# GpSimd's gathers in a factorization-machine kernel: the first layer's products in two halves with four gathers between, in place of eight gathers in a row

## The chip, the cores and the metric

One core of one Trainium2 chip runs the kernel. The metric is the device time of one execution in microseconds (us), lower is better. The kernel before took 1251.6 us, the median of 3 runs (1250.91 to 1251.73).

## The reference

A recommendation tower: 32 embedding lookups per sample, three layers of a compressed interaction network (each multiplies every field of the input with every row of the layer before, and contracts with weights), and a three-layer MLP on the sums.

```python
e = stack([tbl_f[ids[:, f]] for f in range(32)], axis=1)     # 2048 x 32 x 16
x0 = xk = e
for W in (W0, W1, W2):                                       # 32x32x64, 32x64x64, 32x64x64
    xk = relu(einsum('bmd,bhd,mhk->bkd', x0, xk, W))
    outs.append(sum(xk, axis=2))
h = concatenate([concatenate(outs, axis=1), dense_ctx], axis=1)   # 2048 x 208
h = maximum(h @ W_top1 + b_top1, 0)                          # 512
h = maximum(h @ W_top2 + b_top2, 0)                          # 256
y = h @ W_top3
```

All of it is in float32.

## The kernel before, in words

The batch of 2048 is cut into 32 steps of 64 samples. A step's embeddings are a matrix of 32 fields by 1024 columns (64 samples x 16 dimensions). Each engine has a program of its own, written out by hand, and the engines meet at semaphores alone; nothing reorders them.

**How a step's input comes in.** GpSimd (POOL) issues 16 indirect DMAs per step (`gather`, L248), each of which fetches 128 rows of the embedding table into `x_rows`, which is double-buffered. SyncE (SP) waits until all 16 have landed and stores them to a scratch in HBM (`store_x`, L183), twice. When the store has landed (L198) it loads the step back in three groups: `load_a` (L191: four DMAs of 512 KB, chunks 0 to 3 of `spread`), `load_q` (L214: four of 128 KB, the 32 fields four times over in `q_tile`, single-buffered) and `load_b` (L191: four of 512 KB, chunks 4 to 7 of `spread`). `spread` has three buffers. SP's loop is: the B of step s+1, then the store, A and q of step s+2.

**What is computed.** Layer 0 of a step multiplies chunks 0 to 3 of `spread` by `q_tile` into `p_l0` (`first_layer_products`, L260, two GpSimd instructions of two chunks each; ScalarE adds a fifth chunk, the squares, L327). TensorE contracts the five chunks (`layer0`), waiting for `l0_made` chunk by chunk. ScalarE copies the result through a ReLU into `xa` (L300) and `xb` (L309), two arrangements in PSUM, and into `x_s` (L318). VectorE multiplies `spread` with `xa` and `xb` in groups of one to three chunks (`products`, L497): 15 chunks for layer 1, then 15 for layer 2, with the sums over the 16 dimensions (L524) between. The 16th chunk of each of those layers is GpSimd's (`product`, L271). TensorE contracts them (L570).

**The order.** In round s of the loops, VectorE does layer 1 of step s, then layer 2 of step s-1. TensorE does the same, and puts layer 0 of step s+1 after the fourth chunk of layer 2 of step s-1. In every second round the MLP of an earlier pair of steps is put between TensorE's chunks (L632, L634, L644, L652), and ScalarE evicts it (`h`, L414 and L424; `y_row`, L433); its order in the round is `xb` of step s, the third layer's output, `h` of the MLP, `xa` of layer 1 of step s-1, squares, and so on.

**GpSimd's order** is what the change touches. Before the loop it gathers 44 times (`GATHERED_BEFORE`). Then, in round s, it does both instructions of the first layer's products of step s+1, four gathers (`THEN`), the layer-2 product of step s-1, four gathers, the layer-1 product of step s+1, and eight gathers. With 44 + 16 s gathered at the start of the round, the first four gathers of the round complete the rows of step s+2.

Of the kernel before, what the change touches and what calls it, by code (L numbers as in the profile page):

```python
# [6 lines left out]
ALU = mybir.AluOpType  # L7
# [10 lines left out]
Q = P // FIELDS  # L18
SB = 64
STEPS = BATCH // SB  # L20
COLS = SB * DIM
BLK = COLS // 2
XI = COLS // Q // DIM
TILES = BATCH // P
C0 = 5
# [21 lines left out]
L0_AFTER = 3  # L47


GATHERED_BEFORE, THEN = 44, 4  # L50

MLP_AFTER = 5, 10, 13
MLP_AFTER_LAST = 3, 9, 13
# [2 lines left out]
def gathers_before(s):  # L56

    return min(GATHERED_BEFORE + XI * s, XI * STEPS)
# [15 lines left out]
def pool_from(s, layer):  # L74


    if layer == 1:
        return max(0, 2 * s - 1)
    return min(2 * s + 2, 2 * STEPS - 1)


def build_kernel(nc, ids, table, first_row, dense_t, w0_mh, w0_hm, w1, w2, w_top1, b_top1, w_top2,
                 b_top2, w_top3, scratch, y):
    with ExitStack() as ctx:
        def sb(name, shape, dt=F32):
            return ctx.enter_context(nc.sbuf_tensor(name, shape, dt))
# [4 lines left out]
        def sem(name):  # L91
            return ctx.enter_context(nc.semaphore(name))
# [4 lines left out]
        spread = sb("spread", [P, 3, NT, COLS])  # L97
# [4 lines left out]
        p_l0 = sb("p_l0", [P, C0, COLS])  # L102
# [29 lines left out]
        q_loaded = sem("q_loaded")  # L132
        a_loaded = [sem(f"a_loaded{u}") for u in range(3)]
        b_loaded = [sem(f"b_loaded{u}") for u in range(3)]
        l0_made = sem("l0_made")
        squares_made = sem("squares_made")
        l0_used = sem("l0_used")
# [99 lines left out]
        @block.gpsimd  # L237
        def _(pool):
            def gather(n):

                s, i = divmod(n, XI)
                if n == 0:
                    pool.wait_ge(ids_ready, 1)
                if n == FIRST_IDS:
                    pool.wait_ge(ids_ready, 2)
                if i == 0 and s >= 2:
                    pool.wait_ge(x_stored, 32 * (s - 1))
                nc.gpsimd.indirect_dma_start(  # L248
                    out=x_rows[:, s % 2, i * DIM:(i + 1) * DIM], out_offset=None, in_=table,
                    in_offset=bass.IndirectOffsetOnAxis(ap=ids_s[:, n:n + 1], axis=0),  # L250
                ).then_inc(gathered[s % 2], 16)

            def first_layer_products(s):

                pool.wait_ge(q_loaded, 16 * Q * (s + 1))
                pool.wait_ge(a_loaded[s % 3], 16 * Q * (s // 3 + 1))
                pool.wait_ge(l0_used, C0 * s)
                q = q_tile[:].rearrange("p (o n) -> p o n", o=1).broadcast_to([P, 2, COLS])
                for c in 0, 2:
                    nc.gpsimd.tensor_tensor(p_l0[:, c:c + 2, :], spread[:, s % 3, c:c + 2, :],  # L260
                                            q, ALU.mult).then_inc(l0_made, 2)

            def product(s, layer):

                n = pool_from(s, layer)
                pool.wait_ge(x1s_ready if layer == 1 else x2s_ready, s + 1)
                if layer == 1:
                    pool.wait_ge(b_loaded[s % 3], 16 * Q * (s // 3 + 1))
                if n > 0:
                    pool.wait_ge(pool_used, n)  # L270
                nc.gpsimd.tensor_tensor(p_pool[:], spread[:, s % 3, POOL_CHUNK, :], x_s[:, layer - 1, :],  # L271
                                        ALU.mult).then_inc(pool_made, 1)

            def gathers(first, end):

                for n in range(min(first, XI * STEPS), min(end, XI * STEPS)):
                    gather(n)

            gathers(0, gathers_before(0))
            product(0, 1)  # L280
            for s in range(STEPS):
                n = gathers_before(s)
                if s + 1 < STEPS:
                    first_layer_products(s + 1)
                gathers(n, n + THEN)
                if s > 0:
                    product(s - 1, 2)
                gathers(n + THEN, n + 2 * THEN)
                if s + 1 < STEPS:
                    product(s + 1, 1)  # L290
                gathers(n + 2 * THEN, n + XI)
            product(STEPS - 1, 2)

        @block.scalar
# [433 lines left out]
```

## Time and profile before

| | |
|---|---|
| median of 3 runs | 1251.6 us |
| the profiled execution's own time | 1251.98 us |
| its span, first to last instruction | 1250.2 us |
| mean granted TensorE clock | 0.982 of 2.4 GHz |
| busy: TensorE / VectorE / ScalarE / GpSimd | 1127.5 / 1116.6 / 731.7 / 922.8 us |
| gathers (L248) | 512, 955 ns each |
| first layer's products (L260) | 62, 4564 ns each |
| GpSimd's product of layers 1 and 2 (L271) | 64, 2378 ns each |

The span leaves out 1.78 us of the execution's own time (1251.98 - 1250.2). Busy times are of instructions alone; an engine that waits for a semaphore is idle. GpSimd's gathers are the time in which it writes their descriptors; the transfers land later, without an engine's time.

### The profile page before, as it was taken

To read this page: it belongs to the slowest core of one execution; us is meant where nothing else is said; L and a number is where in the kernel's file an instruction comes from. 1 tells how busy PE (TensorE), PEld (TensorE's weight loads), DVE (VectorE), ACT (ScalarE), POOL (GpSimd) and SP (SyncE) were. 2 spreads that over 40 slices of the span, in tenths; PEclk is the share of its full clock that TensorE was granted. 3 is DMA by queue.
4 is the path that set the end of the run, shared out by engine and by line. 5 is a ranking of instruction groups with operands and counts; after the bars stand their busy time and mean duration, and the time that the engine had idled before them with its cause. 6 is when DMAs were issued, how large, how long until landed. Compare 5 with 4: busy or idle time off the path is not lost.

```text
span 1250.2 us, 14620 instructions
## 1 busy us (share of the span) xinstructions
PE 1127.5 (90%) x5312; PEld 395.0 (32%) x5312; DVE 1116.6 (89%) x519; ACT 731.7 (59%) x1361; POOL 922.8 (74%) x642
## 2 busy tenths in 40 slices
PE   0167999999999999999999999999999999999977
PEld 0012323323232333323233332323333332323324
DVE  0159999999999999999999999999999999999992
ACT  0036665766657566765656586565657666565661
POOL 6767888787878878788887878788787878785110
PEclk9888999999999999999999999999999999999988
DMA  5967887657677876666788665667866666777000
GB/s 119 187 132 140 164 164 156 136 117 149 126 148 155 165 145 124 140 126 139 150 164 162 125 145 120 141 133 162 164 142 139 124 142 124 154 163 160 2 1 1
DMA packets 76088, 167.25 MB, mean 134 GB/s; under 512 B 21648, under 2 KB 38944, under 8 KB 76016
## 3 DMA queue, kind: packets, MB, share of 16 engines
q1 hardware_dynamic: 59088, 161.95, 62.0%
q0 software_dynamic: 16384, 4.23, 3.4%
q8 instruction: 42, 0.69, 0.3%
q10 hardware_dynamic: 544, 0.14, 0.1%
q14 instruction: 30, 0.25, 0.1%
HBM read 157.86 MB, written 8.40 MB: 133 GB/s over the span
## 4 chain that ended last, share of the span: by engine, by line
PE 34%; issue 22%; DVE 18%; ACT 14%; another core or an unknown queue 12%; ACTq 0%; DVEq 0%
PE acc L570 30%; DVE p_dve L497 17%; ACT xb L309 10%; PE acc L644 3%; DVE z L524 1%; ACT h L414 1%; PE acc L652 1%; ACT out_l L393 1%; ACT x_s L318 1%; ACT xa L300 0%; PE acc L632 0%; PE acc L634 0%; ACT y_row L433 0%; ACTq L435 0%
## 5 line engine op out<-in xcount | busy, mean ns | idle before, releaser
L570 PE MATMUL acc<-p_dve,w_s 128*64 128x512 f32 x3840 | 868.6, 598 | 65.5 <-DVE p_dve L497 59.5
L248 POOL DMA_INDIRECT x_rows<-in_table,ids_s x512 | 489.2, 955 | 145.9 <-issue 132.9
L497 DVE TENSOR_TENSOR p_dve<-spread,xb 128x3072 f32<-128x3072 f32 (+2 forms) x224 | 565.8, 2583 | 9.8 <-issue 6.7
L497 DVE TENSOR_TENSOR p_dve<-spread,xa 128x2048 f32<-128x2048 f32 (+1 forms) x192 | 495.4, 2634 | 59.6 <-issue 59.6
L570 PEld LDWEIGHTS acc<-p_dve,w_s 128*64 128x64 f32 x3840 | 266.7, 137 | 621.7 <-issue 493.1
L309 ACT ACTIVATE xb<-acc 32x512 f32<-32x512 f32 x512 | 288.8, 564 | 109.4 <-DVE p_dve L497 98.5
L260 POOL TENSOR_TENSOR p_l<-spread,q_tile 128x2048 f32<-128x2048 f32 x62 | 281.3, 4564 | 9.4 <-DMA q_tile<-x_of_steps 8.0
L271 POOL TENSOR_TENSOR p_pool<-spread,x_s 128x1024 f32<-128x1024 f32 x64 | 152.2, 2378 | 137.7 <-ACT x_s L318 84.2
L300 ACT ACTIVATE xa<-acc 64x512 f32<-64x512 f32 x256 | 145.9, 570 | 147.2 <-PE acc L570 109.2
L570 PE MATMUL acc<-p_l,w_s 128*64 128x512 f32 (+1 forms) x640 | 148.9, 601 | 44.6 <-DVE p_l L543 44.6
L318 ACT ACTIVATE x_s<-acc 64x512 f32<-64x512 f32 x256 | 151.3, 591 | 3.8
L414 ACT ACTIVATE h<-acc,bt 128x128 f32<-128x128 f32 x64 | 18.2, 368 | 148.8 <-remote 132.4
L570 PEld LDWEIGHTS acc<-p_l,w_s 128*64 128x64 f32 (+1 forms) x640 | 43.4, 137 | 143.9 <-issue 143.9
L524 DVE TENSOR_REDUCE z<-out_l 128x32 f32<-128x512 f32 x96 | 62.3, 675 | 9.9 <-ACT out_l L393 9.9
L570 PE MATMUL acc<-p_pool,w_s 128*64 128x512 f32 x256 | 65.8, 592 | 0.0
L327 ACT ACTIVATE p_l<-q_tile 32x1024 f32<-32x1024 f32 x32 | 33.6, 1049 | 17.8 <-DMA q_tile<-x_of_steps 16.3
L644 PE MATMUL acc<-h,wt 128*128 128x128 f32 x256 | 34.6, 291 | 7.0 <-ACT h L414 7.0
L644 PEld LDWEIGHTS acc<-h,wt 128*128 128x128 f32 x256 | 31.4, 200 | 20.4 <-ACT h L414 18.8
L570 PEld LDWEIGHTS acc<-p_pool,w_s 128*64 128x64 f32 x256 | 18.4, 137 | 36.5 <-issue 36.5
L632 PE MATMUL acc<-z_all,wt 128*128 128x128 f32 x128 | 27.1, 294 | 3.1 <-ACT z_all L402 3.1
L393 ACT ACTIVATE out_l<-acc 128x512 f32<-128x512 f32 x32 | 19.1, 597 | 15.8 <-PE acc L570 15.3
L543 DVE TENSOR_TENSOR p_l<-spread,q_tile 128x2048 f32<-128x2048 f32 x2 | 4.5, 2288 | 26.6 <-DMA spread<-x_of_steps 26.6
(18 smaller groups left out, 159.8 us busy)
## 6 DMA issues: line engine op xcount, KB each, us to landing
spread<-x_of_steps SPq DMA_DIRECT2D x256, 512.0 KB
q_tile<-x_of_steps SPq DMA_DIRECT2D x128, 128.0 KB
x_rows<-in_table,ids_s POOLq DMA_INDIRECT x512
x_of_steps<-x_rows SPq DMA_DIRECT2D x64, 128.0 KB
w_s<-in_w SPq DMA_DIRECT2D x2, 512.0 KB
wt<-in_w_top SPq DMA_DIRECT2D x1, 512.0 KB
z_all<-in_dense_t ACTq DMA_DIRECT2D x16, 8.0 KB
wt<-in_w_top SPq DMA_DIRECT2D x1, 256.0 KB
```

The source lines that it names most:

```text
L248: nc.gpsimd.indirect_dma_start(out=x_rows[:, s % 2, i * DIM:(i + 1) * DIM], out_offset=None, in_=table, in_offset=bass.IndirectOffsetOnAxi ...
L260: nc.gpsimd.tensor_tensor(p_l0[:, c:c + 2, :], spread[:, s % 3, c:c + 2, :], q, ALU.mult).then_inc(l0_made, 2)
L271: nc.gpsimd.tensor_tensor(p_pool[:], spread[:, s % 3, POOL_CHUNK, :], x_s[:, layer - 1, :], ALU.mult).then_inc(pool_made, 1)
L300: last = nc.scalar.activation(xa[to:to + K, b * BLK:(b + 1) * BLK], acc[b * K:(b + 1) * K, :], ACT.Relu)
L309: last = nc.scalar.activation(xb[q * FIELDS:(q + 1) * FIELDS, b * BLK:(b + 1) * BLK], hi if q % 2 == 0 else lo, ACT.Relu)
L318: last = nc.scalar.activation(x_s[to:to + K, layer - 1, b * BLK:(b + 1) * BLK], acc[b * K:(b + 1) * K, :], ACT.Relu)
L327: nc.scalar.activation(p_l0[0:FIELDS, CP, :], q_tile[0:FIELDS, :], ACT.Square).then_inc(squares_made, 1)
L393: nc.scalar.activation(out_l[:, 2, :], acc2[:], ACT.Relu).then_inc(out_ready[2], 1)
L497: nc.vector.tensor_tensor(p_dve[:, to:to + n, :], spread[:, s % 3, tile:tile + n, :], over(x[:], n), ALU.mult).then_inc(dve_made, n)
L524: nc.vector.reduce_sum(z[:, s // 2 % 2, n, s % 2, :], out_l[:, n, :].rearrange("p (i d) -> p i d", d=DIM), AX_X).then_inc(z_made[n], 1)
L570: last = nc.tensor.matmul(acc[b * K:(b + 1) * K, :], w, prod[:, b * BLK:(b + 1) * BLK], start=start, stop=stop)
L644: last = nc.tensor.matmul(mlp_bank(t)[:, cols], wt2[:, k, cols], h1[:, k, :], start=(k == 0), stop=(k == H1 // P - 1))
```

## The change

The gathers ahead of the loop go from 44 to 40. In a round, the two instructions of the first layer's products stand apart, with four gathers between them, and the row of eight at the round's end becomes a row of four. The first half keeps the three waits; the second has none.

```diff
-GATHERED_BEFORE, THEN = 44, 4
+GATHERED_BEFORE, THEN = 40, 4
...
-            def first_layer_products(s):
-
-                pool.wait_ge(q_loaded, 16 * Q * (s + 1))
-                pool.wait_ge(a_loaded[s % 3], 16 * Q * (s // 3 + 1))
-                pool.wait_ge(l0_used, C0 * s)
+            def first_layer_products(s, c):
+
+                if c == 0:
+                    pool.wait_ge(q_loaded, 16 * Q * (s + 1))
+                    pool.wait_ge(a_loaded[s % 3], 16 * Q * (s // 3 + 1))
+                    pool.wait_ge(l0_used, C0 * s)
                 q = q_tile[:].rearrange("p (o n) -> p o n", o=1).broadcast_to([P, 2, COLS])
-                for c in 0, 2:
-                    nc.gpsimd.tensor_tensor(p_l0[:, c:c + 2, :], spread[:, s % 3, c:c + 2, :],
-                                            q, ALU.mult).then_inc(l0_made, 2)
+                nc.gpsimd.tensor_tensor(p_l0[:, c:c + 2, :], spread[:, s % 3, c:c + 2, :],
+                                        q, ALU.mult).then_inc(l0_made, 2)
...
                 if s + 1 < STEPS:
-                    first_layer_products(s + 1)
+                    first_layer_products(s + 1, 0)
                 gathers(n, n + THEN)
+                if s + 1 < STEPS:
+                    first_layer_products(s + 1, 2)
+                gathers(n + THEN, n + 2 * THEN)
                 if s > 0:
                     product(s - 1, 2)
-                gathers(n + THEN, n + 2 * THEN)
+                gathers(n + 2 * THEN, n + 3 * THEN)
                 if s + 1 < STEPS:
                     product(s + 1, 1)
-                gathers(n + 2 * THEN, n + XI)
+                gathers(n + 3 * THEN, n + XI)
```

GpSimd's program before, one round in the middle of the loop, from one first-layer product to the next (`p_l` is `p_l0`; waits in brackets are the semaphores that the instruction waits for):

```order
L260 TENSOR_TENSOR p_l<-spread,q_tile 128x2048 [waits a_loaded0,l0_used,q_loaded]
L260 TENSOR_TENSOR p_l<-spread,q_tile 128x2048
L248 DMA x_rows<-in_table,ids_s 128x16 x4
L271 TENSOR_TENSOR p_pool<-spread,x_s 128x1024 [waits pool_used,x2s_ready]
L248 DMA x_rows<-in_table,ids_s 128x16 [waits x_stored]
L248 DMA x_rows<-in_table,ids_s 128x16 x3
L271 TENSOR_TENSOR p_pool<-spread,x_s 128x1024 [waits pool_used,b_loaded0,x1s_ready]
L248 DMA x_rows<-in_table,ids_s 128x16 x8
L260 TENSOR_TENSOR p_l<-spread,q_tile 128x2048 [waits a_loaded1,l0_used,q_loaded]
```

The same round in the changed kernel:

```order
L260 TENSOR_TENSOR p_l<-spread,q_tile 128x2048 [waits a_loaded0,l0_used,q_loaded]
L248 DMA x_rows<-in_table,ids_s 128x16 x4
L260 TENSOR_TENSOR p_l<-spread,q_tile 128x2048
L248 DMA x_rows<-in_table,ids_s 128x16 x4
L271 TENSOR_TENSOR p_pool<-spread,x_s 128x1024 [waits pool_used,x2s_ready]
L248 DMA x_rows<-in_table,ids_s 128x16 [waits x_stored]
L248 DMA x_rows<-in_table,ids_s 128x16 x3
L271 TENSOR_TENSOR p_pool<-spread,x_s 128x1024 [waits pool_used,b_loaded0,x1s_ready]
L248 DMA x_rows<-in_table,ids_s 128x16 x4
L260 TENSOR_TENSOR p_l<-spread,q_tile 128x2048 [waits a_loaded1,l0_used,q_loaded]
```

Four of the eight gathers at the round's end now stand between the two halves of the product. The four that complete a step's rows still stand right ahead of the layer-2 product (the gather after that product, which waits for `x_stored`, is the first of the next step).

The end of GpSimd's program ahead of the loop and the first round, before:

```order
L248 DMA x_rows<-in_table,ids_s 128x16 [waits x_stored,ids_ready]
L248 DMA x_rows<-in_table,ids_s 128x16 x11
L271 ISA
L271 TENSOR_TENSOR p_pool<-spread,x_s 128x1024 [waits b_loaded0,x1s_ready]
L260 TENSOR_TENSOR p_l<-spread,q_tile 128x2048 [waits a_loaded1,l0_used,q_loaded]
L260 TENSOR_TENSOR p_l<-spread,q_tile 128x2048
L248 DMA x_rows<-in_table,ids_s 128x16 x4
```

And in the changed kernel:

```order
L248 DMA x_rows<-in_table,ids_s 128x16 [waits x_stored,ids_ready]
L248 DMA x_rows<-in_table,ids_s 128x16 x7
L271 ISA
L271 TENSOR_TENSOR p_pool<-spread,x_s 128x1024 [waits b_loaded0,x1s_ready]
L260 TENSOR_TENSOR p_l<-spread,q_tile 128x2048 [waits a_loaded1,l0_used,q_loaded]
L248 DMA x_rows<-in_table,ids_s 128x16 x4
L260 TENSOR_TENSOR p_l<-spread,q_tile 128x2048
L248 DMA x_rows<-in_table,ids_s 128x16 x4
```

Step 2's rows (the 48th gather) are complete after eight gathers of the first round instead of four. The programs of the other engines are the same in both kernels.

## Rows read from the trace of the kernel before

**Rows 1.** The page: busy time, share of the span, instructions.
```profile
PE 1127.5 (90%) x5312; PEld 395.0 (32%) x5312; DVE 1116.6 (89%) x519; ACT 731.7 (59%) x1361; POOL 922.8 (74%) x642
```
**Rows 2.** Waits of VectorE from 200 to 1100 us: total, times, longest.
```profile
DVE p_dve L497 <- issue: 34.2, 26, 2.3
```
**Rows 3.** Timeline of GpSimd, one round: start, duration, instruction [idle before <-releaser].
```profile
644.78 0.94 POOL L248 DMA_INDIRECT x_rows<-in_table,ids_s  x1 [0.31 <-issue]
645.74 9.06 POOL L260 TENSOR_TENSOR p_l<-spread,q_tile 128x2048 f32<-128x2048 f32 x2
...
658.73 0.95 POOL L248 DMA_INDIRECT x_rows<-in_table,ids_s  x1 [0.30 <-issue]
661.72 2.37 POOL L271 TENSOR_TENSOR p_pool<-spread,x_s 128x1024 f32<-128x1024 f32 x1 [2.04 <-ACT x_s L318]
...
670.93 2.37 POOL L271 TENSOR_TENSOR p_pool<-spread,x_s 128x1024 f32<-128x1024 f32 x1 [1.95 <-PE acc L570]
...
682.24 0.94 POOL L248 DMA_INDIRECT x_rows<-in_table,ids_s  x1 [0.30 <-issue]
683.19 9.08 POOL L260 TENSOR_TENSOR p_l<-spread,q_tile 128x2048 f32<-128x2048 f32 x2
```
**Rows 4.** Timeline of SP's queue in that round: the store, A, and the next B.
```profile
661.06 0.81 SPq L183 DMA_DIRECT2D x_of_steps<-x_rows  x2
663.82 1.74 SPq L191 DMA_DIRECT2D spread<-x_of_steps  x4
...
668.21 1.83 SPq L191 DMA_DIRECT2D spread<-x_of_steps  x4
```
**Rows 5.** Timeline of ScalarE in that round: `xa` of layer 0, the squares.
```profile
663.77 2.31 ACT L300 ACTIVATE xa<-acc 64x512 f32<-64x512 f32 x4 [1.51 <-PE acc L570]
...
678.75 1.06 ACT L327 ACTIVATE p_l<-q_tile 32x1024 f32<-32x1024 f32 x1 [0.50 <-DMA q_tile<-x_of_steps]
```
**Rows 6.** Timeline of SP's queue: the stores of step 3 and of step 31.
```profile
126.72 0.81 SPq L183 DMA_DIRECT2D x_of_steps<-x_rows  x2
...
1130.86 0.81 SPq L183 DMA_DIRECT2D x_of_steps<-x_rows  x2
```
**Rows 7.** Timeline of GpSimd: the first layer's products of steps 1, 3 and 31.
```profile
72.64 9.08 POOL L260 TENSOR_TENSOR p_l<-spread,q_tile 128x2048 f32<-128x2048 f32 x2
...
144.61 4.57 POOL L260 TENSOR_TENSOR p_l<-spread,q_tile 128x2048 f32<-128x2048 f32 x1 [0.47 <-issue]
...
1148.05 9.10 POOL L260 TENSOR_TENSOR p_l<-spread,q_tile 128x2048 f32<-128x2048 f32 x2 [7.97 <-DMA q_tile<-x_of_steps]
```
**Rows 8.** Timeline of TensorE: layer 0's 20 matmuls in the round of rows 3.
```profile
659.12 4.61 PE L570 MATMUL acc<-p_l,w_s 128*64 128x512 f32 x20
```
**Rows 9.** Timeline of VectorE: two like places of early rounds; layer 1 of step 31.
```profile
154.98 8.87 DVE L497 TENSOR_TENSOR p_dve<-spread,xb 128x3072 f32<-128x3072 f32 x4
...
189.60 8.87 DVE L497 TENSOR_TENSOR p_dve<-spread,xb 128x3072 f32<-128x3072 f32 x4
...
1171.87 7.74 DVE L497 TENSOR_TENSOR p_dve<-spread,xa 128x3072 f32<-128x3072 f32 x3
```
**Rows 10.** Timelines of TensorE (its last MLP-1 matmuls) and ScalarE (`h`, two MLPs).
```profile
643.48 0.39 PE L634 MATMUL acc<-z_all,wt 80*128 80x128 f32 x2
...
647.49 0.37 ACT L414 ACTIVATE h<-acc,bt 128x128 f32<-128x128 f32 x1 [10.11 <-remote]
...
1148.12 0.37 ACT L414 ACTIVATE h<-acc,bt 128x128 f32<-128x128 f32 x1 [6.53 <-PE acc L634]
```
**Rows 11.** Windows: length, TensorE busy (matmuls), granted TensorE clock, DMA share, GB/s.
```profile
1211.00:1212.00 1.00, 0.00 (x0) 0.69 0.00 0
...
1219.00:1220.00 1.00, 1.00 (x7) 1.00 0.00 0
```
**Rows 12.** A window of 1 us, all engines; the last two columns are DMA share and GB/s.
```profile
688.00:689.00 1.00, 0.60 (x4) 0.23 (x4) 1.00 (x2) 0.98 (x3) 1.00 (x1) 1.00 0.07 19
```

## The prediction

> **What bounds the kernel now.** The page comes first [rows 1]: TensorE is busy 1127.5 us and VectorE 1116.6 us of a span of 1250.2, GpSimd 922.8. The first two are the pace, and GpSimd looks as if it had a quarter of the time to spare. That share misleads, because GpSimd's gathers also leave gaps of 0.3 us between them, and because it says nothing of what GpSimd waits for and what waits for it. So the second view is GpSimd's timeline over one round [rows 3]. It runs almost without a break: 9.06 us of first-layer products, four gathers, a product, four gathers, a product, eight gathers. The only pauses are 2.04 us for ScalarE's `x_s` and 1.95 us for TensorE's release of `p_pool`.
>
> The third view sets the same round against SP's queue and the landing of `q_tile` [rows 4, 5]. It shows a chain that closes on itself from one round to the next. The four gathers behind the first-layer products complete step s+2's rows. The last one ends at 658.73 + 0.95 = 659.68; the store is issued at 661.06, 1.38 us later; A follows the store and q follows A; ScalarE's squares, which wait for all of q, start at 678.75. GpSimd's first-layer products of the next round need the same q, and start at 683.19. So q was there 4.4 us early.
>
> How long a round is: the products of step 3 start at 144.61 and those of step 31 at 1148.05 [rows 7], which is 1003.44 / 28 = 35.84 us a round. (Rounds with an MLP are longer; the round of rows 3 takes 683.19 - 645.74 = 37.45.) VectorE's own work is 34.62 us a round, the distance of two like places in rounds in which it never stops [rows 9].
>
> **The change part by part.** No instruction is added or removed: 62 halves of first-layer products, 64 products, 512 gathers. Only their order on GpSimd changes, so no busy time enters the sum. What enters is the chain above, because its length is decided by what stands between the start of the first half and the last gather of a step's rows, and that stretch grows.
>
> Stretch one, on GpSimd, from the start of the first half to the end of the gather that completes the rows. Before: two halves, 9.06, and four gathers from 645.74 + 9.06 = 654.80 to 659.68, 4.88: 13.94 us [rows 3]. After: half, four gathers, half, four gathers: 2 x 4.53 + 2 x 4.88 = 18.82 us. The four gathers between the halves are the 4.88 that is added.
>
> Stretch two, from that gather's end to the store: 1.38 us, as it is [rows 3, 4].
>
> Stretch three, from the store to the landing of q. Three places of the trace show it. In rows 4 and 5 it is 678.75 - 661.06 = 17.69. For step 3 GpSimd itself waited: 144.61 - 126.72 = 17.89 [rows 6, 7]. For step 31, with no gathers running beside it, 1148.05 - 1130.86 = 17.19 [rows 6, 7]. It is 2 MB of A and 0.5 MB of q behind a store and its completion, and the change touches none of it: SP's program stays as it is. I take the mean, 17.59, with 17.19 and 17.89 as the ends.
>
> Before, the chain was 13.94 + 1.38 + 17.59 = 32.9 us, below the round of 35.84; it bound nothing. After, it is 18.82 + 1.38 + 17.59 = **37.8 us**, above it (37.4 to 38.1 by the ends). Nothing else in the program can shorten it: the first half of round s+1 needs q of step s+2, that needs the store, the store needs all 16 gathers, and the last four stand behind the second half of round s. Seen from GpSimd: between that last gather and the next first half it had 683.19 - 659.68 = 23.51 us, of which 2.04 + 1.95 were waits and about 5.0 the four gathers that leave (eight take 683.18 - 673.30 = 9.88, four 4.88). That leaves 14.5 us of work against 1.38 + 17.59 = 19.0 of store and load. GpSimd will stand 4.5 us in front of every first half, waiting for q.
>
> Do the gathers land later in the new order? The loads of rows 4 are through at 688 [rows 12], 9 us after q's landing at 678.75. The first half starts with q, so B ends some 9 us into the round, and the gathers that complete the rows are issued from 13.9 us on. They meet idle queues as before; 1.38 stays.
>
> The round before the loop: the 44 gathers become 40, but GpSimd then waited for ScalarE anyway, so I leave the first half of step 1 at 72.64 [rows 7] and count nothing.
>
> Who feels it. TensorE takes a layer-0 chunk in 4.61 / 5 = 0.92 us and needs the second half at 659.12 + 1.84 = 660.96 [rows 8]; it was ready at 654.80, 6.2 us early. A round that is 37.8 - 35.84 = 2.0 us longer eats that within a few rounds, and from then on TensorE stands at chunk 2 of layer 0, ScalarE's `xa` is late, and VectorE waits for it at each layer 1.
>
> **The sum.** The first half of step 30 starts at 72.64 + 29 x 37.8 = 1168.8, its second half ends 4.53 + 4.88 + 4.53 = 13.94 later, at 1182.8. Three chunks of TensorE (2.77) and `xa` (2.31, [rows 5]) follow: VectorE begins layer 1 of step 30 at 1187.9. The last step's two halves have no gathers between them (all 512 are out), so VectorE, not the chain, sets the last round: layer 1 of step 31 starts 34.62 later, at 1222.5. Before it started at 1171.87 [rows 9]. From there to the end the programs are the same, so the span grows by 50.6 us. The profiled execution took 1251.98 us of its own, 0.4 above the median; against the median of 1251.6 the forecast is **1302 us**. With 37.4 and 38.1 us a round it is 12 lower and 9 higher: 1290 to 1311.
>
> **The rivals.**
>
> *The row of eight was the cost (faster).* In the rounds with an MLP ScalarE stands at `h` for about 10 us; TensorE's last matmul for it ends at 643.87, but `h` starts at 647.49 [rows 10], 1.8 us after the eighth gather has ended at 645.72 [rows 3]. Where no gathers run beside it, `h` starts as TensorE ends, at 1148.12 [rows 10]. So a long row of gathers seems to hold `h` back by 3.6 us, and VectorE loses 34.2 us in 26 waits between 200 and 1100 us [rows 2], two in each such round. A row of four would end that: 1251.6 - 34.2 = 1217 us. I believe the gain in the mechanism and not in the time: it counts only if q is there when GpSimd wants it, which asks for a load of 14.5 - 1.38 = 13.1 us after the store, and three places show 17.2 to 17.9. Chance 0.05.
>
> *It changes nothing.* GpSimd would wait for q, but the lateness would not reach TensorE: that needs an excess below 6.2 / 30 = 0.2 us a round, where I find 2.0, or a gain at `h` that happens to equal the loss. 1251.6 us, chance 0.04.
>
> *TensorE's clock falls too (slower still).* TensorE will stand at layer 0 for some us in rounds without an MLP. Near the end of the run it stands idle at 1211, the granted clock falls from 2.4 to 1.2 GHz (0.69 in that window) and is whole again at 1219 [rows 11]. Of these 8 us about 5 are matmuls at half speed, 2.4 us lost. In 15 of the 30 rounds that is 36 us: 1338, if each loss reached the end. Against it: TensorE is not in the chain. Its work is about 1127.5 / 32 = 35.2 us a round [rows 1], so it has 2.6 us of each round to lose before it matters, and GpSimd has 4.5. Chance 0.06.
>
> The Trainium skill (TensorE: Matmul & The Clock Gate, "HAM oscillation — how this bites in real kernels") says that matmul bursts with waits for DMA between them can restart at the low clock every time. The fall at 1211 agrees in kind; by that rule the time would be up to 1338, without it 1302.
>
> **How the numbers follow.** The forecast has 0.85: the chain follows from the order of the programs, and its longest piece was measured three times. Its own bounds are 1290 to 1311; hitches of the queue and a part of the clock rival widen the range upwards, a load that is a little faster in the quieter rounds downwards: 1280 to 1322. Faster by over 0.2% (2.5 us, about what a measurement of this kernel can tell): 0.05, the first rival. Within 0.2%: 0.04. Slower: 0.85 + 0.06 = 0.91.
>
> **What would show it.** Right: the first halves stand 37.4 to 38.1 us apart, each but the first few behind an idle time of about 4.5 us that q's landing ends; TensorE waits for `p_l` at layer 0; VectorE's share of busy time falls to about 86% (1116.6 / 1300); the waits of ScalarE at `h` shrink by some 3.6 us each without a gain. Wrong: first halves that start without a wait for q, or rounds at or below 35.84 us. If the rounds are right and the time still higher, the granted clock shows whether TensorE paid.

## The result, and the profile after

The changed kernel takes 1318.3 us (median of 4 runs, 1315.52 to 1319.32) against 1251.4 for the kernel before: a ratio of 1.0531 [1.0513, 1.055], 67 us more. The direction holds, and the time lies in the widened range of 1280 to 1322; it lies above 1290 to 1311, the bounds that the prediction worked out from its chain, and the forecast of 1302 is 16 us short. The profiled execution took 1319.32 us, its span is 1317.5.

The page of the changed kernel, busy times and the engines of the chain that ended last (compare [rows 1]):

```profile
PE 1154.2 (88%) x5312; PEld 397.4 (30%) x5312; DVE 1119.0 (85%) x519; ACT 731.9 (56%) x1361; POOL 925.3 (70%) x642
...
POOL 34%; DMA 32%; issue 15%; SPq 9%; PE 9%; ACT 2%; DVE 1%; POOLq 0%; ACTq 0%; DVEq 0%
```

VectorE and GpSimd do what they did before, to within 2.5 us, in a span that is 67 us longer, so the time was lost in waiting. TensorE alone is busier, by 26.7 us; the clock, below, accounts for nearly all of that. Two thirds of the chain that ended last are now GpSimd and DMA. The next view, the changed kernel's GpSimd timeline over a round and a half, shows where it stands (compare [rows 3]):

```profile
715.42 0.94 POOL L248 DMA_INDIRECT x_rows<-in_table,ids_s  x1 [0.30 <-issue]
722.07 4.55 POOL L260 TENSOR_TENSOR p_l<-spread,q_tile 128x2048 f32<-128x2048 f32 x1 [5.70 <-DMA q_tile<-x_of_steps]
...
731.51 4.53 POOL L260 TENSOR_TENSOR p_l<-spread,q_tile 128x2048 f32<-128x2048 f32 x1
...
739.98 0.94 POOL L248 DMA_INDIRECT x_rows<-in_table,ids_s  x1 [0.30 <-issue]
740.94 2.37 POOL L271 TENSOR_TENSOR p_pool<-spread,x_s 128x1024 f32<-128x1024 f32 x1
...
761.28 4.57 POOL L260 TENSOR_TENSOR p_l<-spread,q_tile 128x2048 f32<-128x2048 f32 x1 [5.60 <-DMA q_tile<-x_of_steps]
```

Both first halves stand behind q, for 5.7 and 5.6 us. SP's queue in the same round, the store and the loads of A (compare [rows 4]):

```profile
742.32 0.81 SPq L183 DMA_DIRECT2D x_of_steps<-x_rows  x2
744.90 1.75 SPq L191 DMA_DIRECT2D spread<-x_of_steps  x4
```

The three stretches of this round can be read off: from 722.07 to the end of the last gather at 739.98 + 0.94 = 740.92, 18.85 us; to the store at 742.32, 1.40 us; to the next first half at 761.28, 18.96 us. Together 39.21. The chain of waits for this round alone shows the same loop closing on itself (columns: start, duration, what):

```profile
722.07 3.83 POOL p_l L260
...
731.51 4.53 POOL p_l L260
...
739.98 2.32 DMA x_rows<-in_table,ids_s
742.69 0.44 SPq L183
...
748.18 12.97 DMA q_tile<-x_of_steps
761.28 3.83 POOL p_l L260
```

No piece of it belongs to TensorE, VectorE or ScalarE. What they wait for is in the list of waits (total, times, longest):

```profile
POOL p_l L260 <- DMA q_tile<-x_of_steps: 150.7, 31, 12.4
ACT h L417 <- PE acc L637: 101.3, 16, 6.8
DVE p_dve L500 <- PE acc L573: 92.5, 40, 7.2
PE acc L573 <- POOL p_l L260: 59.0, 23, 5.9
```

Every one of the 31 first halves waits for q. TensorE waits for GpSimd's second half at layer 0 (23 times), VectorE in turn for TensorE. The last rounds end as follows in VectorE's timeline: layer 1 of step 30, the wait in the last full round, layer 1 of step 31 (compare [rows 9]):

```profile
1202.07 7.75 DVE L500 TENSOR_TENSOR p_dve<-spread,xa 128x3072 f32<-128x3072 f32 x3 [0.32 <-PE acc L573]
...
1230.92 8.88 DVE L500 TENSOR_TENSOR p_dve<-spread,xb 128x3072 f32<-128x3072 f32 x4 [2.93 <-PE acc L573]
1239.72 5.55 DVE L500 TENSOR_TENSOR p_dve<-spread,xa 128x3072 f32<-128x3072 f32 x2
```

Layer 1 of step 31 starts at 1239.72 where it started at 1171.87 before: 67.9 us later, which is the whole loss.

### The profile page after: what moved, and what is told of

Its sections match the earlier page's. It is cut to its first block, busy times and chain, and to the rows that moved or that the text cites. A ratio compares the mean times of both kernels' runs of the same rounds, so it can differ in the third digit from the quotient of the medians.

```text
span 1317.5 us, 14620 instructions
## 1 busy us (share of the span) xinstructions
PE 1154.2 (88%) x5312; PEld 397.4 (30%) x5312; DVE 1119.0 (85%) x519; ACT 731.9 (56%) x1361; POOL 925.3 (70%) x642
## 4 chain that ended last, share of the span: by engine, by line
POOL 34%; DMA 32%; issue 15%; SPq 9%; PE 9%; ACT 2%; DVE 1%; POOLq 0%; ACTq 0%; DVEq 0%
DMA q_tile<-x_of_steps 26%; POOL p_l L260 18%; POOL x_rows L248 15%; PE acc L573 7%; DMA x_rows<-in_table,ids_s 5%; SPq L191 4%; SPq L214 3%; SPq L183 2%; ACT xb L312 1%; PE acc L647 1%; DVE p_dve L500 1%; DMA x_of_steps<-x_rows 0%; PE acc L635 0%; PE acc L637 0%; ACT x_s L321 0%
## 5 line engine op out<-in xcount | busy, mean ns | idle before, releaser
L573 PE MATMUL acc<-p_dve,w_s 128*64 128x512 f32 x3840 | 874.0, 602 | 53.0 <-DVE p_dve L500 40.6
L248 POOL DMA_INDIRECT x_rows<-in_table,ids_s x512 | 490.2, 957 | 141.7 <-issue 135.9
L500 DVE TENSOR_TENSOR p_dve<-spread,xa 128x2048 f32<-128x2048 f32 (+1 forms) x192 | 495.6, 2636 | 34.2 <-issue 26.3
L260 POOL TENSOR_TENSOR p_l<-spread,q_tile 128x2048 f32<-128x2048 f32 x62 | 282.5, 4556 | 151.2 <-DMA q_tile<-x_of_steps 150.7
L312 ACT ACTIVATE xb<-acc 32x512 f32<-32x512 f32 x512 | 288.8, 564 | 35.7 <-DVE p_dve L500 24.6
L573 PE MATMUL acc<-p_l,w_s 128*64 128x512 f32 (+1 forms) x640 | 172.0, 665 | 103.4 <-POOL p_l L260 59.0
L417 ACT ACTIVATE h<-acc,bt 128x128 f32<-128x128 f32 x64 | 18.2, 368 | 101.3 <-PE acc L637 101.3
L427 ACT ACTIVATE h<-acc,bt 128x128 f32<-128x128 f32 x32 | 10.0, 363 | 50.2 <-PE acc L647 47.3
L396 ACT ACTIVATE out_l<-acc 128x512 f32<-128x512 f32 x32 | 19.1, 598 | 20.6 <-PE acc L573 20.5
```

Of the source, the lines that this page charges most:

```text
L248: nc.gpsimd.indirect_dma_start(out=x_rows[:, s % 2, i * DIM:(i + 1) * DIM], out_offset=None, in_=table, in_offset=bass.IndirectOffsetOnAxi ...
L312: last = nc.scalar.activation(xb[q * FIELDS:(q + 1) * FIELDS, b * BLK:(b + 1) * BLK], hi if q % 2 == 0 else lo, ACT.Relu)
L500: nc.vector.tensor_tensor(p_dve[:, to:to + n, :], spread[:, s % 3, tile:tile + n, :], over(x[:], n), ALU.mult).then_inc(dve_made, n)
L573: last = nc.tensor.matmul(acc[b * K:(b + 1) * K, :], w, prod[:, b * BLK:(b + 1) * BLK], start=start, stop=stop)
```

## The experiments

All are compared with runs of the kernel before on the same chip; those medians lie between 1247.07 and 1251.19 us. First the chain itself: four kernels that make it shorter or longer.

**Four gathers moved ahead of the loop again.** The halves and their order stay as in the changed kernel; only the rows of a step are complete four gathers earlier.

```diff
-GATHERED_BEFORE, THEN = 40, 4
+GATHERED_BEFORE, THEN = 44, 4
```

> The changed kernel with 44 gathers ahead of the loop, as before: the halves stay apart and all rows are of four, but a step's rows are complete after the first four gathers of the round, ahead of the second half. The theory of the chain (first half to last gather of the rows, 1.4 us to the store, 17.9 us to q): 4.55 + 4.88 + 1.5 + 17.9 = 28.8 us, below VectorE's 34.6, so the chain binds nothing. Then 1251 us if a row of eight costs nothing, 1217 if the 34 us that VectorE lost behind h come back. Rival, the split itself is the cost (TensorE waits for a second half that comes 4.9 us later): 1318 us as in the changed kernel.

Measured: 1243.47 us, ratio 0.9972 [0.9953, 0.999]. Stretch one falls to 9.44 us and the whole loss is gone. So neither the halves nor the rows of four cost anything that shows; the loss hangs on when the sixteenth gather of a step comes. The profile also answers the rival on `h` (TensorE's last MLP-1 matmuls, then `h`, then VectorE in the same round):

```profile
639.44 0.39 PE L637 MATMUL acc<-z_all,wt 80*128 80x128 f32 x2
639.86 0.37 ACT L417 ACTIVATE h<-acc,bt 128x128 f32<-128x128 f32 x1 [6.53 <-PE acc L637]
...
654.82 8.88 DVE L500 TENSOR_TENSOR p_dve<-spread,xb 128x3072 f32<-128x3072 f32 x4 [2.19 <-PE acc L573]
```

`h` starts 0.03 us after TensorE has ended (639.83), where it came 3.6 us late before [rows 10]. VectorE still loses 2.19 us in the round, now to TensorE, which is busy without a break from 646 to 656 us with the MLP and the layers: 26.5 us in 12 waits between 200 and 1100 us, where it lost 34.2 in 26 before [rows 2]. Two rounds take 71.51 us, from one `h` to that of the next MLP, 72.12 before. Only some 0.6 us of each MLP comes back, not 2.6 (34.2 us over 13 MLPs). The kernel before shows the same once, in VectorE's timeline of the round in which its `h` is on time (1148.12, [rows 10]):

```profile
1163.07 8.88 DVE L497 TENSOR_TENSOR p_dve<-spread,xb 128x3072 f32<-128x3072 f32 x4 [2.19 <-PE acc L570]
```

**The kernel before with 40 gathers ahead.** Without the halves, so that a step's rows are complete only behind the layer-2 product.

```diff
-GATHERED_BEFORE, THEN = 44, 4
+GATHERED_BEFORE, THEN = 40, 4
```

> The kernel before with 40 gathers ahead of the loop: no split, the row of eight stays, but a step's rows are complete only after the second row of four, behind the layer-2 product. Theory of the chain: 9.06 + 4.88 + 2.4 + 4.88 = 21.2 us and what GpSimd waits for x_s in it, + 1.5 + 17.9 = 40.6 us or more a round against 38.3 in the changed kernel, so 29 x 2.3 = 67 us above it: 1385 us or more. Rival, the split itself is the cost: 1251 us.

Measured: 1383.77 us, ratio 1.112 [1.1056, 1.1183]. GpSimd's first-layer products of two rounds in a row:

```profile
637.90 9.04 POOL L260 TENSOR_TENSOR p_l<-spread,q_tile 128x2048 f32<-128x2048 f32 x2 [7.96 <-DMA q_tile<-x_of_steps]
...
678.27 9.00 POOL L260 TENSOR_TENSOR p_l<-spread,q_tile 128x2048 f32<-128x2048 f32 x2 [6.86 <-DMA q_tile<-x_of_steps]
```

The round is 40.4 us here, and 40.6 on average from step 1 to step 30. So of the change's two parts the start at 40 is what costs, and the split gives back 65 to 69 us of it (1383.77 against 1318.3; the runs were on two chips, and each is 135.9 and 66.9 us above its own kernel before): seen against this kernel the halves are a gain.

**42 gathers ahead**, half way:

```diff
-GATHERED_BEFORE, THEN = 40, 4
+GATHERED_BEFORE, THEN = 42, 4
```

> The changed kernel with 42 gathers ahead of the loop instead of 40: a step's rows are complete two gathers earlier, after two of the four behind the second half. Theory of the chain: 18.89 - 2 x 1.25 = 16.4 us from the first half to the rows, + 1.5 + 17.9 = 35.8 us a round, against 35.76 of TensorE and VectorE (71.51 for two rounds in the kernel with 44): 1242 to 1250 us, so two of the four gathers account for nearly all of the loss. Rival, what costs is that the rows are complete behind the second half at all, whatever the number of gathers: 1318 us.

Measured: 1245.23 us, ratio 1.0006 [0.998, 1.0033]. The stretches have means of 16.44, 1.49 and 17.82 us, 35.7 together, about the round of the kernel before, 35.84. The two gathers more that the changed kernel has in stretch one, 2.45 us, carry it from no loss to a loss of 5%.

**q behind B.** SP loads q last; nothing moves on GpSimd. This lengthens stretch three alone.

```diff
             load_a(1)
+            load_b(1)
             load_q(1)
-            for s in range(STEPS - 1):
-                load_b(s + 1)
-                if s + 2 < STEPS:
-                    store_x(s + 2)
-                    load_a(s + 2)
-                    load_q(s + 2)
+            for s in range(2, STEPS):
+                store_x(s)
+                load_a(s)
+                load_b(s)
+                load_q(s)
```

> The changed kernel with q loaded behind B instead of ahead of it; no load is added. Theory of the chain: 2.1 MB more ahead of q's landing, at 205 KB a us 10.2 us a round: 38.3 + 10.2 = 48.5 us, 1318 + 29 x 10.2 = 1614 us. Rival, q is waited for but something else sets the round: 1318 to 1400 us.

Measured: 1614.16 us, ratio 1.298 [1.2908, 1.3053]. From store to first half it is 27.69 us on average (17.94 in the changed kernel), 9.75 more; times 30 loads that is 292 us, and the time grew by 296. One load of it, SP's queue and then GpSimd:

```profile
724.57 0.81 SPq L183 DMA_DIRECT2D x_of_steps<-x_rows  x2
...
752.27 4.56 POOL L260 TENSOR_TENSOR p_l<-spread,q_tile 128x2048 f32<-128x2048 f32 x1 [12.58 <-DMA q_tile<-x_of_steps]
```

What is put on the chain arrives in the time, microsecond for microsecond.

**A in halves, q between them.** The first half of the products needs chunks 0 and 1 and q only. SP loads those first, then q, then chunks 2 and 3 on a semaphore of their own; GpSimd's second half and VectorE wait for it.

```diff
-                load_tiles(s, 0, NA, a_loaded[s % 3])
+                load_tiles(s, 0, NA // 2, a_loaded[s % 3])
+
+            def load_a2(s):
+
+                load_tiles(s, NA // 2, NA // 2, a2_loaded[s % 3])
...
                     load_a(s + 2)
                     load_q(s + 2)
+                    load_a2(s + 2)
...
                     pool.wait_ge(l0_used, C0 * s)
+                else:
+                    pool.wait_ge(a2_loaded[s % 3], 16 * Q * (s // 3 + 1))
...
                     dve.wait_ge(a_loaded[s % 3], 16 * Q * (s // 3 + 1))
+                    dve.wait_ge(a2_loaded[s % 3], 16 * Q * (s // 3 + 1))
...
```

> The changed kernel with A loaded as two halves: chunks 0 and 1, then q, then chunks 2 and 3; the first half of the product waits for the first and q alone, the second half for the second. Theory of the chain: 1.5 MB instead of 2.5 MB ahead of the first half, at 205 KB a us 5.1 us less: 38.3 - 5.1 = 33.2 us a round, below VectorE's 34.6, so 1217 to 1251 us as in the kernel with 44. Rival, the split or the 40 gathers ahead of the loop are the cost: 1318 us.

Measured: 1236.83 us, ratio 0.9924 [0.9905, 0.9942]. It beats both kernels. GpSimd's wait for q in the whole run:

```profile
POOL p_l L270 <- DMA q_tile<-x_of_steps: 2.5, 1, 2.5
```

One wait of 2.5 us instead of 150.7 in 31. With 1 MB less ahead of q the chain is shorter than the round again, at 40 gathers ahead.

**The same with 44 ahead** asks what the start is worth by itself.

```diff
-GATHERED_BEFORE, THEN = 40, 4
+GATHERED_BEFORE, THEN = 44, 4
```

> The kernel with A in two halves, with 44 gathers ahead of the loop instead of 40. Its chain shrinks by 9.4 us, and binds in neither. If the 6 us that the halves of A gained against the kernel with 44 were won at the start (first half of step 1 on half of A), they stay: 1237 us. If they hang on the 40 gathers ahead of the loop: 1242 us.

Measured: 1243.47 us, ratio 0.9984 [0.9962, 1.0006], the time of the run with 44 and A whole. Once q is early, splitting A brings nothing more; the 6 us between 1236.83 and 1243.47 go with the four gathers fewer ahead of the loop. So with q early, a start of 40 is a gain of some 0.6% and not a loss.

**A row of eight broken in the kernel before** (rows of 4, 8, 4), for the rival on `h`:

```diff
-                gathers(n + THEN, n + 2 * THEN)
+                gathers(n + THEN, n + 3 * THEN)
                 if s + 1 < STEPS:
                     product(s + 1, 1)
-                gathers(n + 2 * THEN, n + XI)
+                gathers(n + 3 * THEN, n + XI)
```

> The kernel before (44, both halves in a row) with the round's gathers as 4, 8, 4 instead of 4, 4, 8: the row of eight stands between the two products, and a row of four runs at the time at which TensorE ends the MLP's first layer. The chain is as before (32.9 us), so it binds nothing. If the length of the row holds h back, h starts as TensorE ends and 34 us come back: 1217 us. If any gather that is running then holds h, h starts about 1.7 us after the last gather of the four, 2 to 4 us late, and the time stays at 1245 to 1251 us.

Measured: 1249.63 us, ratio 1.002 [0.9995, 1.0044]; the 34 us did not come back. ScalarE's `h`, and GpSimd's product behind the row of eight:

```profile
648.98 0.37 ACT L414 ACTIVATE h<-acc,bt 128x128 f32<-128x128 f32 x1 [6.53 <-issue]
```

```profile
639.01 0.94 POOL L248 DMA_INDIRECT x_rows<-in_table,ids_s  x1 [0.30 <-issue]
641.75 2.39 POOL L271 TENSOR_TENSOR p_pool<-spread,x_s 128x1024 f32<-128x1024 f32 x1 [1.80 <-remote]
```

`h` is on time, at most 0.3 us late in any of the 13 MLPs that were late before: here TensorE's last matmul for it ends at 648.95, while a row of four gathers runs (644.28 to 649.00). So a running gather alone does not hold it. But the eight gathers now stand ahead of the layer-1 product, and it is that product which starts 1.80 us after the eighth gather's end; GpSimd's wait for `x_s` grows from 84.2 us in 18 waits to 107.6 in 19. VectorE still waits between 200 and 1100 us, 21.8 us in 23 waits for TensorE and 8.1 in 7 others, 29.9 together where it was 34.2.

What is late can be read from the times at which the trace records the semaphores' updates. In the kernel before, TensorE's last matmul for `h` ends at 643.87, and TensorE has begun its next at 643.79 without a pause; but the update that belongs to that last matmul is recorded at 647.47, and `h` starts 0.02 us after it. In all 13 MLPs whose `h` is late, the update is 3.5 to 3.9 us behind the matmul and 1.6 to 1.8 us behind the eighth gather's end. In the kernel with rows of 4, 8, 4 the late update is TensorE's release of `p_pool`: its matmul ends at 638.38, the update is recorded at 641.59. So it is TensorE's signal that comes late behind a row of eight, not ScalarE that is held, and it delays whoever waits for it.

**A start of 32 gathers, the first product, then 8** (with A in halves), to see whether the long row at the start delays ScalarE's first `xa` as the row of eight delayed `h`:

```diff
-            gathers(0, gathers_before(0))
+            gathers(0, 2 * XI)
             product(0, 1)
+            gathers(2 * XI, gathers_before(0))
```

> The kernel with A in two halves, with GpSimd's 40 gathers ahead of the loop cut in two: 32, then its first layer-1 product, then 8. In every trace so far ScalarE's first copy of layer 0 starts some 4 us after the last gather ahead of the loop (65.5 with 44 gathers, 59.9 to 60.0 with 40), though TensorE's layer 0 of step 0 has ended at about 51. If a long row of gathers holds ScalarE back, it now starts at about 51 and VectorE at about 53 instead of 62; the end moves little, since the first half of step 1 waits for q and GpSimd until 67: 1233 to 1237 us. If something else holds it (the loads, the instruction fetch), it starts at about 60 as before: 1237 us or more.

Measured: 1239.77 us, ratio 0.9908 [0.9892, 0.9925]; the interval overlaps that of 0.9924, so the end gained nothing that shows, where 1233 to 1237 was expected. But the delay is there. ScalarE's first `xa` here:

```profile
52.72 2.31 ACT L314 ACTIVATE xa<-acc 64x512 f32<-64x512 f32 x4 [18.62 <-PE acc L586]
```

and in the kernel before:

```profile
65.50 2.31 ACT L300 ACTIVATE xa<-acc 64x512 f32<-64x512 f32 x4 [31.67 <-remote]
```

Here the 32 gathers end at 43.54, TensorE's layer 0 ends at 52.67 and `xa` starts at once. Before, it ended at 50.62, and `xa` started 14.9 us later, 4.3 us after the 44th gather's end at 61.16; here too the update is recorded late, at 65.48. Against the same kernel with 40 gathers in one row `xa` came 7.2 us earlier (52.72, 59.87 there), and this was lost again: GpSimd's second half came at 79.25 (76.46 there), and TensorE waited 7.36 us for it.

**What made some loads late.** In the changed kernel, 13 of the 30 loads have a packet of an instruction queue (q8) running beside them and took 18.43 us from store to first half on average; the 17 others took 17.57, the forecast's 17.59. The same link stands in three other traces: 18.48 against 17.74 us in the kernel before with 40 ahead, 18.47 against 17.63 and 18.60 against 17.66 in the two kernels below, with 11 such loads of 30 in each. The DMA queues from 717 to 718 us, in the load from 703.29 to 722.07 (packets, MB, share):

```profile
q1 hardware_dynamic: 85, 0.23, 107.1%
q8 instruction: 1, 0.02, 8.2%
```

Two kernels add a transfer of that size to every load, between A and q: 16 KB in one piece, and 17 rows of 1 KB. (The lines that make their tensors and semaphore are not shown.)

```diff
+                if s >= 1:
+                    sp.dma_start(spare[s:s + 1, :], bass.AP(scratch[s, 0:1, :].tensor, scratch[s, 0:1, :].offset, [[4 * COLS, 1], [1, 4 * COLS]])).then_inc(spare_sem, 16)
```

> The changed kernel with one more DMA of 16 KB (one contiguous run, HBM to HBM) on SP's queue between A and q, to copy what TensorE's instruction fetch does, which is one packet of 16 KB. In the changed kernel's trace the 13 loads beside which such a fetch ran took 18.4 us from store to q, the 17 others 17.6. If one packet on one of the 16 DMA engines makes the whole of q late, each round is about 0.9 to 1.3 us longer: 1318 + 26 to 38 = 1344 to 1356 us. If the 16 KB only count as bytes (0.08 us at 205 KB a us), or are spread over the engines: 1318 to 1325 us.

Measured: 1319.18 us, ratio 1.0597 [1.0537, 1.0657], against 1.0531 [1.0513, 1.055] without. No effect that shows: the load's mean is 17.94 us, as without. The trace has 992 packets more, 32 a load, so the 16 KB went out in pieces of 512 bytes and not as one packet.

```diff
+                if s >= 1:
+                    sp.dma_start(spare[s, :, 0:256], scratch[s, 0:17, 0:256]).then_inc(spare_sem, 16)
...
+            sp.wait_ge(spare_sem, 16 * (STEPS - 1))
```

> The changed kernel with one more DMA of 17 rows of 1 KB on SP's queue between A and q. The 16 KB tried before went out as 32 packets of 512 bytes, over all engines, and changed nothing. If 17 rows go to one DMA engine (17 has no divisor up to 16), that engine has 17 KB more to move than the others, at 205 / 16 = 12.8 KB a us 1.3 us, and q is late by as much in every round: 1318 + 29 x 1.3 = 1356 us, or some less where a fetch was the last anyway (1345 to 1356). If the engines share the rest of the work among themselves, or q does not hang on the slowest one: 1318 to 1322 us.

Measured: 1320.5 us, ratio 1.0561 [1.0521, 1.0601]; the load's mean is 18.01 us (17.94). No effect either, and whether one DMA engine carried all 17 rows the trace does not say. So loads beside an instruction packet are late in four traces, but the packet's bytes are not shown to be what delays them; the cause stays open.

## Why the prediction was right, and where it was short

| term | forecast | measured (stretches: mean of 30 rounds) |
|---|---|---|
| stretch one, first half to last gather | 18.82 | 18.89 |
| stretch two, to the store | 1.38 | 1.52 |
| stretch three, store to the next first half | 17.59 | 17.94 |
| round, mean of the 29 from step 1 to step 30 | 37.8 | 38.33 |
| layer 1 of step 31 on VectorE | 1222.5 | 1239.72 |

**The chain** is what bounds the changed kernel, as forecast: the order of its pieces, the wait of GpSimd in front of every first half, TensorE's wait at layer 0, and VectorE's share (85%; 86 forecast) are all there. The experiments that shorten it (44, 42, A in halves) remove the loss, those that lengthen it (q behind B, the kernel before with 40) add what they put on it. The mean round of 38.33 us lies above 38.1, the prediction's upper end for it; the time is in the range only because that was widened for hitches of the queue and for the clock.

**The steps that were short.** Of the 17.2 us that layer 1 of step 31 came later than forecast, 15.4 are the round: 0.53 us, 29 times. The largest part is stretch three, "the mean, 17.59": three loads were taken for thirty, and the highest of the three, 17.89, for the upper end. The measured loads go from 17.10 to 19.03, with 12 above 17.89. None of the three that were taken has a packet of q8 beside it, and the 17 loads of the changed kernel without one have a mean of 17.57; the 13 with one make the difference. The second is stretch two, "1.38 stays": most rounds have 1.3 to 1.5, but four have 1.8 to 2.6; the mean is 0.14 above 1.38, and without these four 0.04. The step "I leave the first half of step 1 at 72.64" was wrong the other way: it came at 69.76, 2.9 us earlier, since ScalarE's first `xa` came earlier behind the shorter row of gathers (60.03 instead of 65.50). The end makes up the rest, 4.7 us: from step 30's first half to its layer 1 on VectorE it took 20.7 us (19.1 forecast), and VectorE's last round took 37.65 instead of "34.62 later", 2.93 of it the wait for TensorE shown above. That term could have been read from the trace before: the last round has an MLP, and in the kernel before it took 1171.87 - 1134.98 = 36.89 us (from layer 1 of step 30), with the wait of 2.19 us at 1163.07 in it.

**The rival on `h`** had the link with the row of eight right and the price wrong. The prediction gave it little chance, but for another reason, that q would not be there. With rows of four the delay is gone, and ScalarE's wait at `h` falls from some 10 to 6.5 us. But "34.2 us" takes waits for their cause: with the delay gone VectorE waits for TensorE in the same rounds, and the kernel with 44 is 4.4 us faster than the kernel before (1247.85 to 1243.47). That the change itself would not have this gain, since q is not there, held.

**The clock rival** came true on TensorE and not in the time. Between 100 and 1200 us the granted clock fell to half in nine places of 3.4 to 10.2 us; in the kernel before it is whole over that stretch but for its first 2 us. One of them, in windows of 2 us (length, TensorE busy, granted clock, DMA share, GB/s), and TensorE's own timeline there:

```profile
1114.00:1116.00 2.00, 0.00 (x0) 1.00 0.07 5
1116.00:1118.00 2.00, 0.00 (x0) 0.53 0.00 0
...
1120.00:1122.00 2.00, 2.00 (x8) 0.50 0.05 4
```

```profile
1119.01 4.82 PE L573 MATMUL acc<-p_l,w_s 128*64 128x512 f32 x12 [5.05 <-POOL p_l L260]
```

TensorE stood 5.05 us at layer 0, the clock went from 2.4 to 1.2 GHz, and the last 12 matmuls of layer 0 took 4.82 us, 2.94 at the full clock. Over the whole run TensorE is busy for 68.6 us at the low clock, 18.0 before; half of the difference, 25.3 us, is nearly all of the 26.7 by which it is busier. The nine rounds in which a fall lies are 38.41 us long on average, the 21 others 38.33: the slow matmuls lie in time in which the chain is elsewhere, as the prediction argued (2.6 us of TensorE's round to lose, 4.5 of GpSimd's).

The Trainium skill (TensorE: Matmul & The Clock Gate, "HAM oscillation — how this bites in real kernels") warns of bursts that restart at the low clock after each wait for DMA. Here the waits are for GpSimd's products, and the trace agrees in nine rounds of thirty; the price in the time, up to 36 us in the prediction, is not seen.

## What to carry to other kernels

An engine with a quarter of its time idle can still close a loop with the queues: follow one buffer once round (computed, stored, loaded, used, refilled) and compare that sum with the round. Here the order of the pieces cost next to nothing while the sum was below the round, and above it every microsecond arrived in the time. Before moving work into such a loop, look for what can be taken out: here q was loaded behind 2 MB of A of which 1 MB was not needed yet. And take a load's duration from many rounds, not three, since in a closed loop its mean counts, and here its spread went upwards.

## What the runs showed of the hardware

Two things were not expected to this extent. Behind a long row of indirect DMAs on GpSimd the semaphore updates of TensorE come late for the engine that waits for them: by 3.5 to 3.9 us for `h` behind a row of eight, by 14.9 us for the first `xa` behind the 44 of the start; rows of four show none of it (`h` starts 0.03 us after TensorE's end). Which path delays them was not found. And a load of 2.5 MB on otherwise like rounds varies by 1.9 us (17.10 to 19.03); 11 of the 12 above 17.89 lie beside a packet of q8, but neither of two transfers of about that size brought it about.
